# Decoder layer on one core: a batch's context keys and values made one body earlier, beside the output norm

## What is computed

```python
def _forward(hidden_states, ...):                      # delta-rule attention
    ...
    o = wgt[..., 0:1] * short + wgt[..., 1:2] * long_ + wgt[..., 2:3] * delta + wgt[..., 3:4] * v
    o = o * jax.lax.rsqrt(jnp.mean(o * o, -1, keepdims=True) + 1e-05) * o_norm_w
    return o.reshape(b, l, H * DV) @ o_proj_w.T

def _L0_xattn_ref(query, key, value, pad_mask, subsq_mask, Wq, bq, Wk, bk, Wv, bv):
    E, H = (256, 16)
    ...
    q = (query @ Wq.T + bq).reshape(n, s, H, d).transpose(0, 2, 1, 3)
    k = (key @ Wk.T + bk).reshape(n, t, H, d).transpose(0, 2, 1, 3)
    v = (value @ Wv.T + bv).reshape(n, t, H, d).transpose(0, 2, 1, 3)
    att = jnp.einsum('bhsd,bhtd->bhst', q, k) / jnp.sqrt(jnp.float32(d))
    ...
    out = jnp.einsum('bhst,bhtd->bhsd', prob, v)

x = x + _L0_attn_ref(_layernorm(x), ...)
x = x + _L0_xattn_ref(_layernorm(x), ctx_1024, ctx_1024, ...)   # the context: 64 rows for each batch
x = x + _L0_ffn_ref(_layernorm(x), ...)
```

## Time and profile before

| | |
|---|---|
| Time, median of 3 runs (lowest to highest) | 1144.95 us (1144.04 to 1145.99) |
| The profiled execution: its time, its span | 1144.12 us, 1142.3 us |
| Mean granted TensorE clock, as a share of full speed | 0.95 |
| PE busy | 997.4 us (87%) |
| DVE, POOL, ACT busy | 803.6, 622.9, 528.2 us |

### The profile page before, as it was taken

The page is one execution under the profiler, slowest core; times in us unless marked ns, Lnnn a source line. Parts: engine busy times, 40 slices in busy tenths (PEclk is TensorE's granted clock), DMA queues, the critical chain, the costliest instruction groups (busy, mean ns, idle before and its releaser), DMA issues.

```text
span 1142.3 us, 26147 instructions
## 1 busy us (share of the span) xinstructions
PE 997.4 (87%) x9538; PEld 733.1 (64%) x9538; DVE 803.6 (70%) x2110; ACT 528.2 (46%) x992; POOL 622.9 (55%) x1009
## 2 busy tenths in 40 slices
PE   4899997887699899899999989989989999988991
PEld 2465657765476676576666667667667667767891
DVE  2879984543676866787677687687678775657487
ACT  2877774513333532542443443353253255755770
POOL 5469898438126636816816735653673215335562
PEclk9999998869799989999989999999999999999996
DMA  9444534450101250260161152122111173224589
GB/s 197 133 163 143 175 93 149 151 157 19 57 20 42 75 151 21 65 185 31 65 183 38 47 141 93 48 70 77 38 55 58 56 266 110 90 89 128 166 286 341
DMA packets 87100, 127.69 MB, mean 112 GB/s; under 512 B 28352, under 2 KB 62784, under 8 KB 84800
## 3 DMA queue, kind: packets, MB, share of 16 engines
q1 hardware_dynamic: 79776, 106.30, 30.2%
q0 software_dynamic: 7200, 19.74, 4.8%
HBM read 66.47 MB, written 59.55 MB: 110 GB/s over the span
## 4 chain that ended last, share of the span: by engine, by line
PE 45%; POOL 20%; DVE 20%; issue 8%; ACT 4%; DMA 1%; SPq 1%; ACTq 0%; DVEq 0%; POOLq 0%
POOL arena L1544 7%; POOL arena L1546 7%; DVE arena L1673 3%; PE bank L562 3%; PE bank L499 3%; PE bank L734 3%; PE bank L468 2%; PE bank L970 2%; POOL orn L1562 2%; PE bank L816 2%; POOL arena L1434 2%; PE bank L576 2%; PE bank L436 2%; PE bank L934 2%; PE bank L588 2%
## 5 line engine op out<-in xcount | busy, mean ns | idle before, releaser
L1044 ACT ACTIVATE arena<-bank 128x512 f32<-128x512 f32 (+4 forms) x358 | 185.9, 539 | 348.8 <-PE bank L961 61.8
L1544 POOL TENSOR_TENSOR arena<-arena 128x126 f32<-128x126 f32 (+22 forms) x248 | 107.0, 432 | 43.9 <-DVE arena L1732 26.1
L1673 DVE SCALAR_TENSOR_TENSOR arena<-arena,param 128x512 f32<-128x512 f32 x144 | 104.1, 777 | 18.8 <-ACT arena L1067 18.1
L1607 POOL DMA_INDIRECT results<-arena x78 | 76.3, 978 | 71.2 <-DVE arena L2225 42.9
L1546 POOL TENSOR_TENSOR arena<-arena 128x126 f32<-128x126 f32 (+22 forms) x248 | 102.2, 412 | 19.4
L419 PE MATMUL bank<-const,arena 128*128 128x128 f32 x256 | 40.5, 310 | 52.7 <-DVE arena L2162 26.7
L1489 POOL DMA_INDIRECT slots_x<-arena x64 | 63.6, 994 | 37.3 <-DVE arena L1964 21.4
L970 PE MATMUL bank<-arena 128*128 128x128 f32 x624 | 83.6, 277 | 0.2 <-ACT arena L1344 0.2
L1513 POOL TENSOR_TENSOR arena<-arena,rb 128x256 f32<-128x256 f32 x32 | 19.7, 616 | 116.5 <-ACT arena L1044 116.0
L970 PEld LDWEIGHTS bank<-arena 128*128 128x128 f32 x624 | 76.9, 194 | 0.4 <-issue 0.4
L1442 POOL COPY arena<-arena 32x128 f32<-32x128 f32 x128 | 53.5, 418 | 38.2 <-DVE arena L1722 31.4
(11 more groups left out here) (293 smaller groups left out, 2635.6 us busy)
## 6 DMA issues: line engine op xcount, KB each, us to landing
arena<-slots_x SPq DMA_DIRECT2D x78, 129.0 KB, 2.1
slots_x<-rows_of_no_token SPq DMA_DIRECT2D x8, 1161.0 KB, 11.7
xt<-x_in SPq DMA_DIRECT2D x16, 512.0 KB, 5.6
kq<-kq_T SPq DMA_DIRECT2D x8, 1024.0 KB, 9.0
arena<-results SPq DMA_DIRECT2D x32, 256.0 KB, 4.8
kq_T<-kq SPq DMA_DIRECT2D x7, 1024.0 KB, 3.9
arena<-ffn_in SPq DMA_DIRECT2D x7, 768.0 KB, 4.1
vT<-v_T SPq DMA_DIRECT2D x8, 514.0 KB, 4.0
```

Of the source, the lines that this page charges most:

```text
L1044: free(act.activation(out_, in_, func, **kw), name)
L1544: own.link(pool.tensor_tensor(tmp, rows32[:, m0:, k].unsqueeze(2).broadcast_to([P, nm, k]), units[:, 0:k, k].unsqueeze(1).broadcast_to([P, ...
L1607: pool.indirect_dma_start(results[:, :], bass.IndirectOffsetOnAxis(ap=dest[:, n % YS:n % YS + 1], axis=0), ys[:, n % YS, :], None).then_in ...
L1673: ins = V.scalar_tensor_tensor(cv[:, k % 4, :], pre[:, j, d:d + GT], param[:, at:at + 1], cv[:, k % 4, :], ALU.mult, ALU.add)
```

## The change

The context of batch b moves from the head of body 2b + 1 to the tail of body 2b, on three engines at once: on PE behind the first `late_out` and ahead of the wait for `on_ready`, on ACT behind the router's activation, on DVE behind the second `late` and ahead of the wait for `orms_ready`, that is for POOL's powers. SP gets one more wait (`mask_ready`) ahead of the load of the next context. Nothing else differs. In the listings below the line numbers of the changed kernel are 2 to 5 lower than those of the kernel before.

```diff
@@ PE, body
                 pair_corner(i)
-                if x:
-                    context()
                 half_inner(i)
...
                     late_out(i - 1, (2, 3), (0,))
+                if i % G == 0:
+                    cross(i)[0]()
                 pe.wait_ge(sem("on_ready"), i + 1)
                 transpose_rows(om, [f"oT0.{i}", f"oT1.{i}"], (next(body_bank), next(body_bank)))
@@ ACT, body
                 pair_inner(i)
-                if x:
-                    keys()
                 pair_corner(i)
...
                 if x and not ahead:
                     tile_experts(0)
+                if i % G == 0:
+                    cross(i)[0]()
                 for c in range(CK):
                     n = f"oT{c}.{i}"
@@ DVE, body
                     rows2()
                     masks()
-                    context()
                     anykey()
...
                     if x:
                         late((k,))
+                if i % G == 0:
+                    cross(i)[4]()
                 for k in range(2):
                     dve.wait_ge(sem("orms_ready"), 2 * i + k + 1)
@@ SP
                     if i % G == 1:
                         sp.wait_ge(sem("kblk_ready"), i // G + 1)
+                        sp.wait_ge(sem("mask_ready"), i)
                         load_context(i // G + 1)
```

More of the change, by code:

```diff
@@ L530, in context @@
                 def context():
-                    if g:
-                        return
                     pe.wait_ge(sem("ctx_loaded"), 48 * (b + 1))
@@ L1145, in keys @@
                 def keys():
[L1146 to L1152, removed]
+                    n = f"kx.{b}"
+                    o = filled(act, n)
+                    for m in range(CK):
+                        last = act.activation(kxT[:, m, :], o[:, m * S2:(m + 1) * S2], ACT.Identity,
+                                              bias=prm("bk", m, 1))
+                    free(last, n)
                 def rows():
```

## The result

The changed kernel takes 1163.22 us (median of 4 runs, 1161.86 to 1165.6), the kernel before 1144.49 us beside it: 1.63% slower, ratio 1.0163 (95% interval 1.0142 to 1.0184). The profiled execution of the change took 1165.6 us with a span of 1163.8 us. It is the slowest of the four, so its trace shows 21.5 us more than that of before, where the medians show 18.7.

A forecast was written before the change was run, and what follows sets the result against it. PE was busy 87% of the span, with DVE the chain at even tails. Tails 10.2 + tail clock 0 + odd heads 3.4 = 13.6 us on 1144.12 gave 1157.7, plus 0.8 for the median: 1158 us, range 1150 to 1163.

The forecast's parts named there:

- The tails, DVE's part: Tails of bodies 2, 4, 6: DVE waits for `vx`, then its context instructions delay the ranks; 3.4 us each, 10.2 in all.
- The tails, the clock: Tails of bodies 2, 4, 6: PE's longer idle stretch may lower the clock; bounds 0 to 0.95 us each, taken as 0.
- The odd heads: Heads of bodies 1, 3, 5, 7: without the context the clock falls as in even heads; +0.86 us each, 3.4 in all.
- The even heads: Heads of even bodies: already at low clock, 16.51 us in body 2, used as template for odd heads; no term of their own.
- Tails with a low clock: Rival: the clock falls in the tails as well, adding 2.9 us to the forecast; 1161 us, chance 0.15.
- The heads keep the clock: Rival: same tails, but the four odd heads stay at full clock and shorten by 1.05 us each; 1151 us, chance 0.21.
- Faster: Rival: if `vx` is there when DVE is free, a tail costs 0.3 us and heads get shorter; 1142 us, chance 0.04.
- The rule that I set against the trace: Odd heads: clock falls need much longer PE idle gaps, so they would keep full clock and the change cost 6.0 us.

The follow-up runs named there:

- e4: The changed kernel with three dummy products on PE in the even tails, in the wait behind the context: 1157.4 us, ratio to before 1.0123.
- e1: The changed kernel with DVE's four context instructions back in the odd heads, PE's and ACT's parts staying at the tail: 1152.81 us, ratio to before 1.0085.
- e7: The changed kernel with PE's context in the tails of bodies 2, 4 and 6 moved ahead of the first `late_out`: 1155.1 us, ratio to before 1.0099.
- e2: The changed kernel with six context-shaped dummy products on PE at the context's old place in the odd heads: 1156.86 us, ratio to before 1.0128.
- e5: The changed kernel with DVE's context back at the odd heads and six dummy products in the heads of bodies 1 to 7: 1138.32 us, ratio to before 0.9957.
- e3: The kernel before with six dummy products added in the heads of bodies 2, 4 and 6: 1142.43 us, ratio to before 0.9994.
- e8: The changed kernel with PE's context ahead of the first `late_out` and dummy products in the heads of bodies 1 to 7: 1140.07 us, ratio to before 0.9952.
- e6: The changed kernel with DVE's context back at the odd heads and only two wide dummies in each head of bodies 1 to 7: 1139.44 us, ratio to before 0.9951.

## Why the prediction was wrong

It was 13 us over the median before, with a range up to 1163 us; the median came out at 1163.2, 18.7 us over. The direction and, but for the even heads, the places were right; the sum was too small, and the clock is what was undersized. By the trace the terms are: DVE's part of the tails 9.0 us (forecast 10.2), the clock in the tails 3.5 (0), the odd heads 5.5 (3.4), the even heads 4.1 and the tail of body 1 -1.0 (neither in the sum), together 21.1 against 13.6.

*The tails, DVE's part* (forecast 3.4 us each): right in mechanism, and 0.4 us too large. DVE stood 2.98 us at `vx`, the ranks came 3.4 us later after the late product than before (forecast 3.76), POOL's 0.35 us were recovered, and with the clock held (e4) a tail costs 3.0 us. e1 and e7 show that it is DVE's wait and not PE's work.

*The tails, the clock* ("I take 0 for the sum, since the context itself gives PE work in that stretch"): **this step failed**. In the profile all three even tails went to 1.2 GHz, 1.15 us each, 3.5 in all; my bounds were 0 to 0.95, and the two long tails of e2, 16.62 us against 14.18 in e4, show 2.4. The context came ahead of an idle stretch of 3.36 us and did not cover it. e4 covers it, and wins the 1.15 us in each.

*The odd heads* (forecast 4 x 0.86 = 3.4 us): the mechanism was right and is shown by e2 and e5, the size was not. The heads lost 1.83, 1.38, 1.34 and 0.93 us, 5.5 in all, and nothing took it back, since the middles stayed as they were. I had taken the even body as a template down to its last multiplication; but from the solved rows on, an odd body is longer by 571.08 - 503.63 - (479.41 - 412.52) = 0.56 us, in both kernels. I subtracted that difference from the loss, though nothing removes it. The length of the heads themselves was forecast well: 16.5 us, measured 16.26 to 16.47.

*The even heads* (not in the sum): +4.1 us in the profile, through a low stretch of 9.5 us in place of 6.3. Nothing in their code changed. In all profiles together, heads with neither context nor dummies in which the clock fell 3.2 to 3.5 us behind the opening addition took some 18.0 us, those in which it fell at 3.7 to 5.1 us took 16.2 to 16.9, two in which it fell at 5.3 us 15.3, and the one in which it did not fall (e2, body 4) 14.05. So this term hangs on when the fall comes, which the change shifted. That the shift is a lasting effect and not the luck of the profiled execution is not settled: e7 shows 18.0 us in all three even heads, e1 in one of three, and the profiled execution of the change is the slowest of its four.

*The rivals.* Tails with a low clock came true, on top of the forecast's own terms. "The heads keep the clock" fell: all four odd heads went low; its price was right, for the bare head of e2 that kept the clock takes 14.05 us, and 15.09 - 1.05 = 14.04 was forecast. "Faster" named its condition rightly: with `vx` made earlier (e7) a tail costs 0.7 us, of which 0.44 is what DVE still waits for `vx`; the rest agrees with the forecast 0.3. The rule that I set against the trace (the Trainium skill, "TensorE: Matmul & The Clock Gate", section "HAM oscillation — how this bites in real kernels", which lays the fall to idle gaps) goes the right way for the even tails, where the clock fell as the gap grew to 3.36 us. It does not fit the tail of body 1, where the clock fell in the kernel before with a pause of 1.74 us (e7's even tails kept it with 1.73), nor the heads, where it fell with a longest pause of 0.74 us before it.

*What is open.* Where the clock fell in the runs without a trace, and so how much of the 18.7 us of the medians each term makes. Times spread by 4 us in the change and by 9 in the kernel before (1139.95 to 1149.18), and the mean granted clock of each run goes with them: in the kernel before it is 0.957 in the fastest of 25 runs and 0.948 in one of 1148.67 us, in the change 0.939 at 1161.86 us and 0.933 at 1165.6, which is the profiled one. So the clock's terms in that trace are probably larger than in a median run. The traces of e2, e3 and e5 show falls that come and go at places with the same code.

## What to carry to other kernels

Work that moves into an engine's idle wait is free on that engine alone: look at each engine that takes part, and above all at the one whose list holds the chain, since a wait put ahead of the chain costs nearly its whole length (2.54 us of wait made 2.3 us of tail, e4 against e7) even where the instructions behind it are hidden. Before taking "needless" products off TensorE, compare a stretch with them and one without in the same trace: here the head with less work was the longer one, and 2 us of dummy products made it 1.9 us shorter. A template from another part of the trace should be compared piece by piece, so that a difference that stays is not booked as a gain.

## What the runs showed of the hardware

TensorE's clock fell to 1.2 GHz in stretches where PE was hardly idle but did hardly more than 32x32 and 64x64 products: in 33 of the 34 heads of these traces that have neither context nor dummies, with a longest pause of 0.75 us before the fall. Of the 29 heads with 2 us of full-width products among them (context or dummies) 28 stayed at 2.4 GHz (before, e2, e3, e5, e8). Two wide products, 0.9 us, held it in five heads of seven (e6). What it is in these products that holds the clock is not shown: they are wide, and they also close the pause of 0.74 us. No run put small products in their place. Against the pause speaks the one head of the 29 that fell, body 7 in e3: its longest pause in that stretch was 0.40 us.

The fall is not tied to a place: this head of body 7 kept the clock in the kernel before and lost it in e3, and the head of body 4 lost it in every trace in which it has no dummies but that of e2. The Trainium skill, "TensorE: Matmul & The Clock Gate", section "What's actually happening", says of a kernel's start that the number of products at the low clock varies from run to run. For whole executions the record agrees: the mean granted clock of the 25 runs of the kernel before lies between 0.948 and 0.957.
